# Second mixture of a two-layer transformer kernel: gate and up of the first 512 tokens move ahead of two turned groups and the router's products

## The chip, the cores and the metric

The kernel runs on one core of a Trainium2 chip. The metric is the device time of one launch in microseconds (us), given as the median over runs. A profile is one execution taken by the hardware profiler. Its engines are PE (matmuls; PEld are its weight loads), ACT (ScalarE), DVE (VectorE), POOL (GpSimd) and SP, the queue that issues the DMAs. L86 means line 86 of the kernel.

## The reference, cut to what matters

Two layers, each an attention and a mixture of experts, with a layer norm behind each of the four parts. Activations are 2 x 1024 tokens of 256 features, float32. The part touched here is what lies between the attention of the second layer and its mixture:

```
x = _layernorm(x + _L1_attn_ref(x, ...), axis=-1)
# _L1_ffn_ref:
scores = xf @ gate_w.T
probs = jax.nn.softmax(scores.astype(jnp.float32), axis=-1)
_, idx = jax.lax.top_k(probs + gate_b, TOP_K)          # 6 of 16 experts
h = jax.nn.silu(xf @ W1.T + B1) * (xf @ W3.T + B3)     # each expert, and the shared one
out = h @ W2.T + B2
```

## The kernel before, in words

**Data.** Features lie on the 128 partitions, tokens along the free axis. Every float32 operand of a product is split into a rounded high part and a remainder (`xh`, `xl`; `hi_gu`, `lo_gu`), and `mm3` forms each product as three matmuls (L86, L87, L88). ACT rounds (copies) and DVE subtracts to get the remainder; for weights POOL does the subtraction (L1190).

**A mixture.** `mixture` is called twice, as "f0" for the first layer and "f1" for the second. It runs over `2 * NT` tiles of hidden units K (the two halves of 1024 tokens one after the other), and for each K over NC = 2 chunks c of 512 tokens. PE's order for a (K, c) is `gate(K, c)`, `up(K, c)` (twelve matmuls together), then `down(K - 1, c)`, then the side tasks that `plan` names for this place. ACT does silu, DVE the product with up (`f_hid`, L1473), ACT the rounding (`f_hh`, L1422), DVE the remainder (`f_hl`, L1484). `gate(0, 1)` waits for silu of (0, 0), and `up(0, 1)` for the product of (0, 0), as there is one bank of PSUM for gate and one for up.

**Side tasks.** The norm and the router of 1024 tokens are cut into tasks, each with a part on PE (`tensor`), ACT (`scalar`) and DVE (`vector`), and each engine does its parts in program order. Engines meet through the semaphores of a ring: `filled` by PE, `rounded` by ACT, `emptied` by DVE. The tasks that count here:
- `root`: ACT takes the square root (L212), DVE the reciprocal (L223) and then normalises eight blocks of 128 tokens into `yT` (L227). Each block is counted on `xn_done`.
- `nb` s, s = 0 to 3: 256 tokens, called a group here, are turned back so that features lie on partitions. PE does four 128x128 turns (L204), ACT copies them to `xh` (L217), DVE subtracts to `xl` (L241) and counts `emptied`.
- `lg` c: the router's scores of 512 tokens, six matmuls with `g_rw_gwh` and `g_rw_gwl`. PE waits until `nb` 2c + 1 is emptied. DVE copies the result out (L389).
- `lt`: PE turns the scores (eight small turns, L347); it waits until the copy of `lg` 1 is done. DVE goes on with the maximum (L392 to L395).

**The start of f1.** What is called `lead` in the program, and `fore` inside `mixture`, is the list `root`, `nb` 0 to 3, `lg` 0, `lg` 1. With `ready` = 0, PE does all of it ahead of the loop over K, then gate and up of (0, 0), then `lt`, the first task of `plan[0, 0]`, and then gate of (0, 1). ACT does `root`, rounds the first weights (L1186), and then does its parts of the other six tasks, loads the table of silu (L1435), rounds `b2` (L1438) and goes on to silu (L1411). DVE does all its parts of the list, then `b2l` (L1492), then the product of (0, 0).

In the call for f0 (`ready` = 2, `split` = 2) PE does two tasks of `fore` ahead of the loop and the rest behind gate and up of (0, 0).

Of the kernel before, what the change touches and what calls it, by code (L numbers as in the profile page):

```python
# [1190 lines left out]
                           ALU.subtract).then_inc(self.lo_done, 1)  # L1191


def mixture(nc, tag, counters, w, gu, ready, xh, xl, yT, idr, eps, psum, shared_gate, routers, fore, split, plan, after, begins=(), store=None):

# [9 lines left out]
    with Phase(nc, tag, psum) as ph:  # L1207
# [42 lines left out]
        fore_ring = Ring(counters, side_banks + [o for row in y_banks for o in row] + [up_ps, gate_ps])  # L1250
# [65 lines left out]
        @block.tensor  # L1316
        def _(pe):
            def gate(K, c):
                if c == 0:
                    pe.wait_ge(gu.lo_done, K + 1)  # L1320
                if K * NC + c >= 1:

                    pe.wait_ge(silu_done, K * NC + c)
                elif fore_ring.last(gate_ps):
                    pe.wait_ge(fore_ring.emptied, fore_ring.last(gate_ps))
                for dt in range(DT):
                    w0 = dt * P
                    i = mm3(pe, gate_ps, hi_gu[:, K % 2, w0:w0 + P], lo_gu[:, K % 2, w0:w0 + P],
                            xh[:, dt, tokens(K, c)], xl[:, dt, tokens(K, c)], dt == 0, dt == DT - 1)
                i.then_inc(gate_done, 1)  # L1330

            def up(K, c):
                if K * NC + c >= 1:

                    pe.wait_ge(prod_done, K * NC + c)
                elif fore_ring.last(up_ps):
                    pe.wait_ge(fore_ring.emptied, fore_ring.last(up_ps))
                for dt in range(DT):
                    w0 = (DT + dt) * P
                    i = mm3(pe, up_ps, hi_gu[:, K % 2, w0:w0 + P], lo_gu[:, K % 2, w0:w0 + P],  # L1340
                            xh[:, dt, tokens(K, c)], xl[:, dt, tokens(K, c)], dt == 0, dt == DT - 1)
                i.then_inc(up_done, 1)

            def begin_y(K, c):
                half = K // NT
                if half:

                    pe.wait_ge(y_kept, (c + 1) * DT)
                for dt in range(DT):
                    if not half and fore_ring.last(y_banks[dt][c]):  # L1350
                        pe.wait_ge(fore_ring.emptied, fore_ring.last(y_banks[dt][c]))
                    pe.matmul(y_banks[dt][c], idr[:], xh[:, dt, tokens(K, c)], start=True, stop=False)
                    pe.matmul(y_banks[dt][c], idr[:], xl[:, dt, tokens(K, c)], start=False, stop=False)

            def bias_y(K, c):
                r, x = routers[K // NT], slice(c * CH, (c + 1) * CH)
                pe.wait_ge(b2_lo, 1)
                for dt in range(DT):
                    d = slice(dt * P, (dt + 1) * P)
                    mm3(pe, y_banks[dt][c], b2h[:, d], b2l[:, d], r.cTh[:, x], r.cTl[:, x], False, False)  # L1360

            def down(K, c):
                if c == 0:
                    pe.wait_ge(lo_dn_done, K + 1)
                pe.wait_ge(hlo_done, K * NC + c + 1)
                for dt in range(DT):
                    d0 = dt * P
                    i = mm3(pe, y_ps[:, dt, c, :], hi_dn[:, K % 2, d0:d0 + P], lo_dn[:, K % 2, d0:d0 + P],
                            hh[:, K % 2, c, :], hl[:, K % 2, c, :], False, K % NT == NT - 1)
                i.then_inc(down_done, 1)  # L1370

            for side, t in fore[:split] if ready else fore:
                side.tensor(pe, t, fore_ring)
            for K in range(2 * NT + 1):
                for c in range(NC):
                    if K <= LAST:
                        gate(K, c)
                        up(K, c)
                    if ready and K == 0 and c == 0:
                        for side, t in fore[split:]:  # L1380
                            side.tensor(pe, t, fore_ring)
                    if K >= 1:
                        if (K - 1) % NT == 0:
                            begin_y(K - 1, c)
                        if biased and (K - 1) % NT == nsh:
                            bias_y(K - 1, c)
                        down(K - 1, c)
                    for side, t in plan.get((K, c), ()):
                        side.tensor(pe, t, ring)
# [509 lines left out]
def program(nc, a, out):  # L1899
    with ExitStack() as stack:  # L1900
# [5 lines left out]
        xh = sb("xh", [P, DT, T], F32R)  # L1906
        xl = sb("xl", [P, DT, T], F32R)
        yT = sb("yT", [P, DT, T])
        ident = sb("ident", [P, P])
        idr = sb("idr", [P, P], F32R)  # L1910
        eps = sb("eps", [P, 1])
        psum = stack.enter_context(nc.psum_tensor("psum", [P, 8, CH], F32))
        rows = out.rearrange("b s d -> (b s) d")
        counters = Counters(nc, stack)
# [8 lines left out]
        def maps(r):  # L1923
            return ([(r, ("ct", c)) for c in range(S // CH)] +
                    [(r, ("cm", c, m)) for c in range(S // CH) for m in range(r.rw.nmap)])
# [16 lines left out]
        def place(first, slots):  # L1942
# [3 lines left out]
        w0 = {"groups": 1, "shared_tiles": NSH0, "topk": 2, "gate_w": a["gw0"], "gate_b": None, "sel": a["sel0"],  # L1946
              "gu": a["gu0"], "bias": a["bias0"], "down": a["down0"]}
# [4 lines left out]
        with Phase(nc, "g") as g:  # L1952
# [19 lines left out]
            with Phase(nc, "x") as x:  # L1972
                wqkv = Projection(x, "wqkv", a["wqkv1"], a["bqkv1"])
                x.level(0)
                ks = [x.sb("ks0", [P, 2, S], F32R)]
                vs = [x.sb("vs0", [P, S // P, G1, VW])]
                qhi = [x.sb("qhi0", [P, 2, S], F32R)]
                qlo = [x.sb("qlo0", [P, 2, S], F32R)]
                with Phase(nc, "s0") as s:
                    n0b, n1a = norm(s, "n0b", 1), norm(s, "n1a", 0)  # L1980
                    r0b = router(s, "r0b", 1, rw0, "n0b")
                    kv, khi, klo = s.sb("kv", [P, S]), s.sb("khi", [P, S], F32R), s.sb("klo", [P, S], F32R)
                    x0 = QKVHalf(s, "x0", 0, wqkv, kv, khi, klo, xh, xl, ident, "n1a").into(qhi[0], qlo[0], ks[0], vs[0])
                    plan = {**place(0, norm_slots(n0b) + PAUSE + router_slots(r0b)),
                            **place(NT0 + 1, norm_slots(n1a) + PAUSE + tasks(x0, PROJECT))}
                    for c, t in enumerate(maps(r0a)[3::2]):
                        plan[3, c] = plan.get((3, c), []) + [t]
                    mixture(nc, "f0", counters, w0, gu0, 2, xh, xl, yT, idr, eps, psum, True, (r0a, r0b), maps(r0a)[:2] + maps(r0a)[2::2], 2, plan, n1a, (wqkv, x0))

                ks.append(x.sb("ks1", [P, 2, S], F32R))  # L1990
                vs.append(x.sb("vs1", [P, S // P, G1, VW]))
                qhi.append(x.sb("qhi1", [P, 2, S], F32R))
                qlo.append(x.sb("qlo1", [P, 2, S], F32R))
                x.level(0)
                queries = Queries(x, "queries", qhi, qlo)
                with Phase(nc, "s1") as s:
                    n1b = norm(s, "n1b", 1)
                    kv, khi, klo = (o[:].rearrange("p s n -> p (s n)") for o in (raw_gu, hi_gu, lo_gu))
                    x1 = QKVHalf(s, "x1", 1, wqkv, kv, khi, klo, xh, xl, ident, "n1b").into(qhi[1], qlo[1], ks[1], vs[1])
                    in_turn(nc, "p1", counters, psum, tasks(n1b, FORE + [("root",)] + BACK) + tasks(x1, PROJECT), (x1, wo, rw1, queries))  # L2000
                    o1a = OutHalf("o1a", 0, wo, z[0], qhi[0], qlo[0], xh, xl, yT, ident, idr)
                    follows(n2a, o1a)
                    order = [TURN[0], TURN[1], GATHER[0], GATHER[1], TURN[2], TURN[3], GATHER[2], GATHER[3]]
                    rear = list(zip((1, 2, 4, 6, 8, 9, 11, 13, 15, 17, 19, 21), tasks(o1a, order) + tasks(n2a, FORE)))
                    grouped_attention(nc, "a1", counters, queries, (x0, x1), ks, vs, z, ident, psum, rear)

            with Phase(nc, "s2") as s:
# [12 lines left out]
                        **place(NSH1, tasks(o1b, TURN) + PAUSE + tasks(o1b, GATHER) + PAUSE + norm_slots(n2b) + PAUSE +  # L2020
                                router_slots(r1b)),
                        **place(NT1 + 1, norm_slots(n3a, False))}
                mixture(nc, "f1", counters, w1, gu1, 0, xh, xl, yT, idr, eps, psum, False, (r1a, r1b), lead, 1, plan, n3a, (),
                        (n3a, rows, stored, 0))
            n3b = norm(g, "n3b", 1)
            in_turn(nc, "p3", counters, psum, tasks(n3b, FORE + [("root",)]), (), (n3b, rows, stored, NormHalf.GROUPS))
# [86 lines left out]
```

## Time and profile before

| | us |
|---|---|
| median of 3 runs | 2165.48 (2164.84 to 2167.04) |
| the profiled execution | 2165.89 |
| its span, first to last instruction | 2163.9 |
| PE busy in it | 2092.4 |
| mean granted clock of PE | 0.984 of full |

Times in the rows are in us from the start of the span. A row of the timeline gives the start, the duration, the engine, the line, the operation, what is written and read, the shape and the count; in square brackets stands how long the engine had been idle and which instruction released it. Matmuls overlap, so the distance between two starts is what one costs.

### The profile page before, as it was taken

What the parts mean: (1) busy time and instruction counts of PE and PEld (TensorE: products, weight loads), DVE (VectorE), ACT (ScalarE), POOL (GpSimd) and SP (SyncE); (2) the same over time, 40 slices, a digit from 0 to 9 for tenths busy, and PEclk for the clock granted to TensorE, in tenths of its full rate; (3) what the DMA queues carried; (4) which work ended last, traced back from release to release, by engine and by line L of the source; (5) the groups of instructions that cost most, each with busy time, mean ns of one, the idle gap of its engine ahead of it and who ended that gap; (6) DMA issues with size and microseconds to landing.
All of it is one profiled execution on the core that took longest, in us unless ns stands there. A gap on an engine that the chain in (4) does not pass through costs nothing. (4 is left out here: it accounts for less than half of the span.)

```text
span 2163.9 us, 31289 instructions
## 1 busy us (share of the span) xinstructions
PE 2092.4 (97%) x11136; PEld 1595.3 (74%) x11136; DVE 1454.1 (67%) x2761; ACT 1211.4 (56%) x2435; POOL 576.7 (27%) x679
## 2 busy tenths in 40 slices
PE   7999999999999999989999989999999899999997
PEld 6888888888788888877788863333334678778886
DVE  5666666667666776666656568888885556655555
ACT  5666666666556666644444444778777534444433
POOL 3444444444334444422222210000000112222221
PEclk9999999999999999999999986999999999999999
DMA  2000000000000000011111120000000111111111
GB/s 74 20 21 19 14 21 20 21 20 20 9 20 21 21 20 21 16 30 39 45 44 45 44 50 14 20 18 22 16 22 2 43 37 44 44 44 39 50 52 56
DMA packets 54301, 64.78 MB, mean 30 GB/s; under 512 B 9179, under 2 KB 34566, under 8 KB 54150
## 3 DMA queue, kind: packets, MB, share of 16 engines
q1 hardware_dynamic: 54150, 62.81, 10.4%
q8 instruction: 90, 1.47, 0.3%
q14 instruction: 61, 0.50, 0.1%
HBM read 52.68 MB, written 2.10 MB: 25 GB/s over the span
## 5 line engine op out<-in xcount | busy, mean ns | idle before, releaser
L862 POOL TENSOR_TENSOR a_pr<-a_pr,a_rinv 128x512 f32<-128x512 f32 (+3 forms) x384 | 312.2, 827 | 476.4 <-DVE a_rinv L1109 476.4
L86 PE MATMUL psum<-xh,g_hi_gu 128*128 128x512 f32 x928 | 377.7, 407 | 16.2 <-DVE xl L1092 10.0
L88 PE MATMUL psum<-xh,g_lo_gu 128*128 128x512 f32 x928 | 363.3, 392 | 0.0
L87 PE MATMUL psum<-xl,g_hi_gu 128*128 128x512 f32 x928 | 362.6, 391 | 0.0
L1817 DVE TENSOR_REDUCE a_negm<-psum 128x1 f32<-128x1024 f32 x256 | 301.6, 1220 | 37.5 <-PE psum L1688 36.8
L1190 POOL TENSOR_TENSOR g_lo_gu<-g_raw_gu,g_hi_gu 128x512 fp32r<-128x512 f32 x84 | 108.6, 1292 | 793.3 <-ACT g_hi_gu L1186 793.3
L1796 ACT ACTIVATE a_pt<-psum 128x512 f32<-128x512 f32 x512 | 269.2, 603 | 85.5 <-PE psum L1703 85.0
L1484 DVE TENSOR_TENSOR f_hl<-f_hid,f_hh 128x512 fp32r<-128x512 f32 x168 | 116.9, 696 | 238.6 <-ACT f_hh L1422 236.6
L1411 ACT ACTIVATE f_act_s<-psum,g_gu_bias 128x512 f32<-128x512 f32 x168 | 115.0, 684 | 277.4 <-PE psum L88 277.1
L1014 ACT ACTIVATE a_pr<-psum,a_negm 128x128 f32<-128x128 f32 (+7 forms) x256 | 190.0, 742 | 106.8 <-DVE a_negm L1099 102.6
L1021 ACT ACTIVATE a_pth<-psum 128x512 fp32r<-128x512 f32 (+3 forms) x384 | 174.7, 489 | 113.2 <-PE psum L921 107.9
L86 PEld LDWEIGHTS psum<-xh,g_hi_gu 128*128 128x128 f32 x928 | 174.8, 188 | 56.8 <-issue 14.4
L88 PEld LDWEIGHTS psum<-xh,g_lo_gu 128*128 128x128 f32 x928 | 174.5, 188 | 38.4
L1116 DVE TENSOR_TENSOR a_ptl<-psum,a_pth 128x512 fp32r<-128x512 f32 (+3 forms) x384 | 201.1, 551 | 1.5 <-ACT a_pth L1021 1.2
L87 PEld LDWEIGHTS psum<-xl,g_hi_gu 128*128 128x128 f32 x928 | 175.3, 189 | 31.8
L1422 ACT ACTIVATE f_hh<-f_hid 128x512 fp32r<-128x512 f32 x168 | 105.5, 628 | 157.7 <-DVE f_hid L1478 153.6
L1688 PE MATMUL psum<-x_ks,x_queries_qq 48*128 48x512 f32 x512 | 185.9, 474 | 7.9 <-DVE a_negm L1817 4.7
L1099 DVE CUSTOM_DVE_ANT_0 psum<-psum,a_mask 128x128 f32<-128x128 f32 (+7 forms) x256 | 191.7, 749 | 1.5 <-PE psum L88 0.2
L921 PE MATMUL psum<-ident,a_pr 128*128 128x128 f32 x1152 | 170.5, 275 | 9.8 <-DVE a_ptl L1116 7.0
L1703 PE MATMUL psum<-x_queries_qq,x_ks 49*128 49x512 f32 x512 | 171.5, 481 | 0.9 <-ACT a_pt L1796 0.4
L1703 PEld LDWEIGHTS psum<-x_queries_qq,x_ks 49*128 49x128 f32 x512 | 68.4, 188 | 133.1 <-ACT a_pt L1796 127.2
L921 PEld LDWEIGHTS psum<-ident,a_pr 128*128 128x128 f32 x1152 | 134.3, 140 | 33.0 <-POOL a_pr L862 21.3
(298 smaller groups left out, 4310.0 us busy)
## 6 DMA issues: line engine op xcount, KB each, us to landing
g_raw_gu<-in_gu SPq DMA_DIRECT2D x84, 256.0 KB, 2.7
f_raw_dn<-in_down SPq DMA_DIRECT2D x84, 128.0 KB, 2.0
g_raw_gu<-in_qkv SPq DMA_DIRECT2D x32, 256.0 KB, 2.9
a_wvr<-in_qkv SPq DMA_DIRECT2D x32, 128.0 KB, 2.3
a_wor<-in_o SPq DMA_DIRECT2D x32, 128.0 KB, 2.0
x_queries_qq<-x_qhi SPq DMA_DIRECT2D x128, 32.0 KB, 2.0
yT<-in_xT SPq DMA_DIRECT2D x4, 512.0 KB, 6.6
x_queries_qq<-x_qlo SPq DMA_DIRECT2D x64, 32.0 KB, 2.0
```

Of the source, the lines that this page charges most:

```text
L86: pe.matmul(out, a_hi, b_hi, start=first, stop=False)
L87: pe.matmul(out, a_hi, b_lo, start=False, stop=False)
L88: return pe.matmul(out, a_lo, b_hi, start=False, stop=last)
L862: pool.tensor_tensor(x, x, rinv[:, j:j + 1].to_broadcast([P, count * P]), ALU.mult).then_inc(p_done, 1)
L921: i = pe.transpose(t_ps[:, n % 2, k * P:(k + 1) * P], pr[qt % NP][:, (k0 + k) * P:(k0 + k + 1) * P], ident[:])
L1014: act.activation(split(qt, pr[qt % NP][:, 0:n]), scored(qt), ACT.Exp, bias=negm[:, qt % NP:qt % NP + 1], scale=-1.0, accum_out=rsum[:, qt ...
L1099: dve.tensor_tensor_reduce(x, x, split(qt, mask[:, S - (qt + 1) * P:S]), -1.0, 3.0e38, ALU.add, ALU.min, negm[:, qt % NP:qt % NP + 1]).the ...
L1116: dve.tensor_tensor(ptl[c][:, p, :], t_ps[:, n % 2, 0:count * P].rearrange("p (k q) -> p k q", q=P), pth[c][:, p, :].bitcast(F32), ALU.sub ...
L1688: m = pe.matmul(mx_ps[:, bank, half, :], qq[p0:p0 + ROWS, u % QSLOT, g % 2, q * P:(q + 1) * P], ks[b][p0:p0 + ROWS, g % 2, half * CH:(half ...
L1703: pe.matmul(st_ps[:, n % 3, :], ks[b][p0:p0 + ROWS + 1, g % 2, kt * P:(kt + 1) * P], qq[p0:p0 + ROWS + 1, u % QSLOT, g % 2, :], start=True ...
L1796: act.activation(pt[:, s % SLOTS, g, :], st_ps[:, n % 3, :], ACT.Exp, scale=1.0 / HD1).then_inc(exp_done, 1)
L1817: dve.tensor_reduce(negm[:, u % 2, g * NQ + q:g * NQ + q + 1], mx_ps[:, bank, :, :], AX.XY, ALU.max, negate=True).then_inc(mx_taken, 1)
```

## The change

`mixture` gets a parameter `ahead`: how many tasks of `fore` PE does before the loop over K. The rest follow gate and up of (0, 0) in both calls. For f0 `ahead` is 2, as `split` is, so its order stays; the added wait is only issued where the last task ahead is an `nb`, and there it is a `ct`. For f1 `ahead` is 3: `root`, `nb` 0 and `nb` 1 stand ahead, then PE waits until DVE has emptied `nb` 1 (tokens 0 to 511 are complete then), then come gate and up of (0, 0), and behind them `nb` 2, `nb` 3, `lg` 0, `lg` 1 and `lt`. The orders of ACT, DVE, POOL and SP are not edited; `split` still divides ACT's list.

```diff
-def mixture(nc, tag, counters, w, gu, ready, xh, xl, yT, idr, eps, psum, shared_gate, routers, fore, split, plan, after, begins=(), store=None):
+def mixture(nc, tag, counters, w, gu, ready, xh, xl, yT, idr, eps, psum, shared_gate, routers, fore, split, ahead, plan, after, begins=(), store=None):
...
-            for side, t in fore[:split] if ready else fore:
+            for side, t in fore[:ahead]:
                 side.tensor(pe, t, fore_ring)
+            for side, t in fore[:ahead][-1:]:
+                if t[0] == "nb":
+                    pe.wait_ge(fore_ring.emptied, fore_ring.count((side.name, t)))
             for K in range(2 * NT + 1):
                 for c in range(NC):
                     if K <= LAST:
                         gate(K, c)
                         up(K, c)
-                    if ready and K == 0 and c == 0:
-                        for side, t in fore[split:]:
+                    if K == 0 and c == 0:
+                        for side, t in fore[ahead:]:
                             side.tensor(pe, t, fore_ring)
...
-                    mixture(nc, "f0", counters, w0, gu0, 2, xh, xl, yT, idr, eps, psum, True, (r0a, r0b), maps(r0a)[:2] + maps(r0a)[2::2], 2, plan, n1a, (wqkv, x0))
+                    mixture(nc, "f0", counters, w0, gu0, 2, xh, xl, yT, idr, eps, psum, True, (r0a, r0b), maps(r0a)[:2] + maps(r0a)[2::2], 2, 2, plan, n1a, (wqkv, x0))
...
-                mixture(nc, "f1", counters, w1, gu1, 0, xh, xl, yT, idr, eps, psum, False, (r1a, r1b), lead, 1, plan, n3a, (),
+                mixture(nc, "f1", counters, w1, gu1, 0, xh, xl, yT, idr, eps, psum, False, (r1a, r1b), lead, 1, 3, plan, n3a, (),
```

## Rows read from the trace of the kernel before

**Rows 1.** The page: busy tenths of PE in 40 slices, and its granted clock.

```profile
PE   7999999999999999989999989999999899999997
...
PEclk9999999999999999999999986999999999999999
```

**Rows 2.** PE's waits over the span: for what, us in total, times, longest.

```profile
PE psum L204 <- DVE yT L227: 8.6, 3, 4.6
```

**Rows 3.** Timeline of PE at the start of f1, and DVE's first product.

```profile
1690.59 1.97 PE L204 MATMUL psum<-ident,yT 128*128 128x128 f32 x8 [3.69 <-DVE yT L227]
...
1692.88 1.97 PE L204 MATMUL psum<-ident,yT 128*128 128x128 f32 x8 [0.32 <-DVE yT L227]
...
1694.81 0.58 PE L86 MATMUL psum<-xh,g_rw_gwh 128*16 128x512 f32 x1
...
1696.05 0.40 PE L86 MATMUL psum<-xh,g_rw_gwh 128*16 128x512 f32 x1
...
1697.90 0.39 PE L88 MATMUL psum<-xh,g_rw_gwl 128*16 128x512 f32 x1
...
1700.62 0.39 PE L88 MATMUL psum<-xh,g_lo_gu 128*128 128x512 f32 x1
...
1700.94 0.67 PE L347 MATMUL psum<-ident,yT 16*128 16x16 f32 x8
...
1701.12 0.75 DVE L1473 SCALAR_TENSOR_TENSOR f_hid<-psum,g_gu_bias,f_act_s 128x512 f32<-128x512 f32 x1 [1.78 <-PE psum L88]
...
1701.54 0.50 PE L86 MATMUL psum<-xh,g_hi_gu 128*128 128x512 f32 x1
```

**Rows 4.** Timeline of POOL, DVE and ACT in the same stretch.

```profile
1691.40 1.27 POOL L1190 TENSOR_TENSOR g_lo_gu<-g_raw_gu,g_hi_gu 128x512 fp32r<-128x512 f32 x1 [419.73 <-ACT g_hi_gu L1186]
...
1693.39 1.96 DVE L241 TENSOR_TENSOR xl<-psum,xh 128x512 fp32r<-128x512 f32 x3
...
1694.88 0.60 ACT L217 ACTIVATE xh<-psum 128x512 fp32r<-128x512 f32 x1 [0.26 <-PE psum L204]
...
1695.49 1.28 ACT L1435 ACT_TABLE_LOAD   x1
1695.51 0.69 DVE L241 TENSOR_TENSOR xl<-psum,xh 128x512 fp32r<-128x512 f32 x1 [0.16 <-ACT xh L217]
...
1698.33 0.68 DVE L389 COPY yT<-psum 16x512 f32<-16x512 f32 x1 [0.69 <-PE psum L88]
```

**Rows 5.** Timeline of the stage before the grouped attention, turns and ACT's copies.

```profile
1268.81 1.94 PE L198 MATMUL psum<-ident,yT 128*128 128x128 f32 x16 [1.43 <-PEq L54]
...
1269.47 2.06 ACT L217 ACTIVATE yT<-psum 128x512 f32<-128x512 f32 x4 [0.97 <-PE psum L198]
...
1275.33 3.68 PE L204 MATMUL psum<-ident,yT 128*128 128x128 f32 x16 [4.59 <-DVE yT L227]
```

**Rows 6.** Stretches: length, busy per engine (instructions), PE's granted clock, DMA share, GB/s.

```profile
1279.60:1280.00 0.40, 0.40 (x3) 0.32 (x3) 0.32 (x1) 0.04 (x1) 0.00 (x0) 0.96 0.28 56
1290.00:1337.00 47.00, 40.00 (x100) 16.95 (x102) 38.63 (x35) 10.10 (x20) 0.00 (x0) 0.53 0.14 25
...
1689.00:1690.00 1.00, 0.00 (x0) 0.00 (x0) 0.41 (x2) 0.51 (x2) 0.00 (x0) 0.62 0.77 274
...
1696.00:1697.00 1.00, 1.00 (x6) 0.41 (x5) 0.25 (x2) 0.99 (x3) 0.00 (x0) 0.97 0.00 0
...
2149.50:2156.80 7.30, 3.54 (x22) 2.72 (x22) 2.87 (x13) 5.20 (x9) 0.00 (x0) 1.00 0.00 0
```

**Rows 7.** Timeline of PE at the kernel's start.

```profile
10.03 0.77 PE L86 MATMUL psum<-xh,g_hi_gu 128*128 128x512 f32 x1 [10.03 <-DVE xl L1092]
...
13.15 0.46 PE L87 MATMUL psum<-xl,g_hi_gu 128*128 128x512 f32 x1
...
13.45 0.39 PE L88 MATMUL psum<-xh,g_lo_gu 128*128 128x512 f32 x1
```

**Rows 8.** The stretch from gate of (0, 1) to nearly the end of f1.

```profile
1701.50:2150.00 448.50, 443.96 (x1974) 358.65 (x1974) 256.76 (x434) 186.75 (x335) 100.32 (x99) 1.00 0.15 45
```

## The prediction

> **What bounds the kernel now.** I read four views. First the page: the matmul engine (PE) is at 9 tenths in nearly every slice, so a change pays only where PE idles, and costs wherever it puts an idle stretch in front of PE [rows 1]. Second, PE's waits over the whole run: the second largest is the one for `yT` from L227, the normalised rows which the turning back needs, 8.6 us in three places [rows 2]. The second mixture `f1` begins with one of them. Third, the timeline of PE there [rows 3]: groups 0 and 1 are turned from 1690.59, groups 2 and 3 from 1692.88, and the router's twelve products (`lg`, 16 columns of weights, but 512 moving columns) start at 1694.81. They are followed without a gap by gate and up of the first 512 tokens, by `lt` at 1700.94 and by gate of the second 512 tokens, G, at 1701.54. Fourth, the other engines in that stretch [rows 4]. VectorE (DVE) forms `xl` of groups 0, 1 and 2 back to back from 1693.39 (three in 1.96 us, so 0.64 apart); group 1's ends at 1693.39 + 0.64 + 0.68 = 1694.71. PE starts 0.1 us behind that. So what ends PE's wait is DVE's second subtraction, and two things lie under it for nothing: the turns of groups 2 and 3, which PE does while DVE is busy, and, under the later lg products, ScalarE's (ACT's) copies and DVE's subtractions of these groups. Likewise DVE's copy of the second lg result (1698.33 to 1699.01) lies under gate and up. I follow one mark, G: from there on the order on every engine is unchanged.
>
> **The change, part by part.** In the first mixture the third and later tasks stay where they were, and the new wait isn't issued (the task ahead is no `nb`): 0. In `f1` no product, copy, transfer or byte is added. SyncE's and GpSimd's queues are untouched. One semaphore wait is added on PE, for DVE's subtraction of group 1. Queued behind it are now gate, up, and then everything else of PE. Before, `lg` 0 waited for the very same event, so gate can't start before 1694.81, and its weights are ready (GpSimd is done at 1691.40 + 1.27 = 1692.67) [rows 4]. Gain from an earlier start of PE: nothing. What changes is what is covered.
>
> Step 1, twelve gate and up products from 1694.81. At full clock they are 0.227 us apart ((1700.62 - 1697.90) / 12). If the clock rises when it did before, three steps take 1.24 us (1694.81 to 1696.05), the other eight 1.82, and the last starts at 1697.87. The next task starts 0.32 later, as `lt` did (1700.62 to 1700.94): T = 1698.19 [rows 3].
>
> Step 2, groups 2 and 3 are turned from T, now alone. At full clock sixteen turns take 1.94 us, so eight take about 0.95; ACT's first copy starts 0.66 after the first turn, and four copies take 2.06, so they are 0.49 apart [rows 5]. The second copy ends at T + 0.66 + 0.49 + 0.60 = T + 1.75. DVE follows 0.03 behind each (as at 1695.51), 0.64 apart and 0.68 long: done at T + 2.61. PE follows 0.07 later, so `lg` 1 starts at T + 2.68. `lg` 0 covers part of it (from T + 0.97, six products at 0.23, to T + 2.35); 0.33 us stay open.
>
> Step 3, `lg` 1: five steps, with 0.1 for the first one after a wait, put its last product at T + 3.93. DVE's copy starts 0.43 behind it (1697.90 to 1698.33) and takes 0.68: T + 5.04. `lt` needs it and has no cover now: it starts at about T + 5.1, and G comes 0.60 later, at T + 5.7 [rows 3, 4]. PE waits some 1.0 us here, where it waited for nothing before.
>
> Step 4, ACT and DVE behind the moved tasks. ACT ends the copies at T + 1.75, loads the table (1.28), does the two small ones, and is free at about T + 3.5, before the silu of G is needed; silu ends at T + 4.2. DVE has the first product behind both lg copies and `b2l`: about T + 5.35, which is 0.35 before G, where before it was 0.42 before G (1701.12) [rows 3]. Nothing new is late: 0, but nothing is won either.
>
> At the old clock the sum is G = 1698.19 + 5.7 = 1703.9, that is 2.35 later: about 0.95 for the turns, 0.33 and 1.0 for the two open waits, the rest for restarts. A lower bound of this part is 1.3 (both waits hidden somehow), the upper one 2.6.
>
> Step 5, the clock. PE is at the lower of its levels (1.2 GHz) from 1689.2 (the mean of 0.62 in the slice from 1689 puts the fall there), after it stood idle behind the attention, and at 2.4 GHz from 1696.0 [rows 6]. It had then been turning and multiplying since 1690.59, 5.4 us with two gaps of 0.3. After the change PE turns two groups, then stands for 2.3 us until 1694.81. Three rises give the bounds: 3.1 us after the first product at the kernel's start (10.03 to 13.15), 4.3 after the first turn in the stage before the grouped attention (1275.33 to 1279.6), and 5.4 here [rows 5, 6, 7]. Counted from 1694.81 that is 1697.9, 1699.1 or 1700.2. A slow step takes 0.41 here and 0.45 at the kernel's start; I use 0.42. The middle value makes eleven of the twelve products slow: last start 1694.81 + 10 x 0.42 + 0.38 = 1699.4, T = 1699.7, G = 1705.4, 3.85 us later than before. The early one gives T = 1699.2 and 3.3; the late one all twelve slow, and half-rate turns behind them, 4.3.
>
> The rule that bears on it is in the Trainium skill, "TensorE: Matmul & The Clock Gate", Part 1: the slow level is the default, and only sustained work releases the fast one. The rows of rises agree; by it the sum is the 3.85 above. Its Part 4 says more: a turn doesn't count as work for the clock. By this the rise would stay where it was, and the sum be 2.35. That is the second rival.
>
> The sum is +3.8 us. The profiled execution took 2165.89 us for a span of 2163.9, and stands 0.4 above the median of 2165.48. On the median the forecast is 2169.3; the new profile should show a span near 2167.7. A difference of 0.2% (4.3 us) is about what a measurement of this kernel can tell from no change, so this loss most likely counts as none.
>
> **Rivals.**
> A, the forecast: cover lost and clock late, +3.3 to +4.3.
> B, the clock rises as early as before. For it: counted from the first ordinary product, the rise came 1.2 us later here (1694.81 to 1696.0) and in the earlier stage it came 0.6 us after the sixteen turns had ended (1275.33 + 3.68 = 1279.0, to 1279.6). Against it: from 1290 to 1337 PE was busy 85% with ordinary products and the clock stayed at 0.53, so a short run of products is not enough; and at the kernel's start it took 3.1 us [rows 5 to 7]. Time: 2165.48 + 2.35 = 2167.8.
> C, the clock rises and then falls again in the new waits (0.33 and 1.0 us, with tiny turns between). The stay at the low level here lasted 6.8 us (1689.2 to 1696.0); a second one costs 6.8 x (1 - 0.227 / 0.42) = 3.1. Time 2165.5 + 3.8 + 3.1 = 2172.4, slower. Against it: at 2149.5 to 2156.8 PE was busy only half of the stretch (3.54 of 7.30) and kept the full clock; the new stretch is busier [rows 6].
> D, the other side: the loss is given back. Silu of the first tokens is done 1.5 us before G, so ACT and DVE could run ahead of PE, and the waits that PE has later in this mixture (448.50 - 443.96 = 4.54 us idle) would shrink [rows 8]. If all go, -4.5 + 3.8 = -0.7: 2164.8. It decides from the point where more than 3.8 of the 4.5 vanish. Against it: DVE's first product stays behind the lg copies (step 4), 0.35 before G instead of 0.42, and both engines are in order from there.
> E, the change has less effect than it seems, because the turns of groups 2 and 3 overlap gate and up somehow: excluded, as PE issues in program order and they stand behind `up`.
>
> **How the numbers follow.** A 0.74, B 0.13, C 0.09, D 0.04. Faster by over 0.2%: a part of D and scatter, 0.03. Slower: C (0.09) and the upper third of A, since 4.3 is its late end and runs of one kernel spread by 2 us (2164.84 to 2167.04): 0.25; together 0.34. Within 0.2%: 0.63. The likeliest is 2169.3. The range takes in B's time with some scatter below, 2167.0, and A's late end with scatter and a part of C above, 2171.3.
>
> **What would show it.** In the new profile: PE's first gate product of `f1` at the place where lg was, 1.3 us after DVE's first L241; a wait of PE of some 2.3 us ahead of it in place of 0.3 and 0.3; the turns of groups 2 and 3 about 4.9 us behind it, about 1 us long; `lt` 5.1 us behind the turns with a wait for DVE's L389 of about 1.0; and G 10.6 us behind the first gate product (6.73 from the first lg product before). The granted clock should rise 3 to 5.5 us after the first gate product. From G to the end the time should be unchanged within 0.5 us (462.4 us before, 2163.9 - 1701.54). The prediction is wrong if gate starts earlier than DVE's second subtraction, if the copy L389 doesn't delay `lt`, if the clock rises within 2 us, or if the idle time of PE after G changes by more than 1 us.

## The result, and the profile after

The changed kernel takes 2170.45 us (median of 16 runs, 2167.51 to 2172.82), the kernel before 2166.4 us (16 runs, 2164.84 to 2167.87). The ratio is 1.0017, 95% interval 1.001 to 1.0023: 4.05 us more, where 3.8 were forecast. The profiled execution took 2170.44 us for a span of 2168.4. Two executions far out of line, 8848.66 us in the first experiment and 5099.13 us of the kernel before beside it, are in no ratio and no spread given below, and no trace shows what they did.

First the timeline of PE in the changed kernel, with ACT's square root on top. It answers to [rows 3].

```profile
1689.14 0.30 ACT L212 ACTIVATE g_n2a_std<-g_n2a_mv,eps 128x8 f32<-128x8 f32 x1
...
1690.51 1.97 PE L204 MATMUL psum<-ident,yT 128*128 128x128 f32 x8 [3.70 <-DVE yT L227]
1694.59 0.79 PE L86 MATMUL psum<-xh,g_hi_gu 128*128 128x512 f32 x1 [2.12 <-DVE xl L241]
1695.18 0.63 PE L87 MATMUL psum<-xl,g_hi_gu 128*128 128x512 f32 x1
...
1699.45 0.63 PE L88 MATMUL psum<-xh,g_lo_gu 128*128 128x512 f32 x1
1699.88 1.47 PE L204 MATMUL psum<-ident,yT 128*128 128x128 f32 x8
1701.10 0.47 PE L86 MATMUL psum<-xh,g_rw_gwh 128*16 128x512 f32 x1
...
1703.01 0.39 PE L86 MATMUL psum<-xh,g_rw_gwh 128*16 128x512 f32 x1 [0.28 <-DVE xl L241]
...
1704.16 0.39 PE L88 MATMUL psum<-xh,g_rw_gwl 128*16 128x512 f32 x1
1705.41 0.64 PE L347 MATMUL psum<-ident,yT 16*128 16x16 f32 x8 [0.86 <-DVE yT L389]
1705.98 0.50 PE L86 MATMUL psum<-xh,g_hi_gu 128*128 128x512 f32 x1
```

The order is the new one. The brackets name three waits that the change brought: 2.12 us for DVE's second subtraction (L241), 0.28 for its fourth, and 0.86 for the copy of the second router result (L389). All twelve gate and up products have a duration of 0.63 or more and, behind the first, stand 0.43 apart, so all of them are slow. The mark G, gate of the second 512 tokens, stands at 1705.98.

Next ACT and DVE behind the moved tasks, from the same timeline. It answers to [rows 4].

```profile
1700.94 1.09 ACT L217 ACTIVATE xh<-psum 128x512 fp32r<-128x512 f32 x2 [7.83 <-PE psum L204]
...
1701.58 1.29 DVE L241 TENSOR_TENSOR xl<-psum,xh 128x512 fp32r<-128x512 f32 x2 [7.04 <-ACT xh L217]
...
1704.59 0.68 DVE L389 COPY yT<-psum 16x512 f32<-16x512 f32 x1 [1.14 <-PE psum L88]
...
1705.53 0.73 DVE L1476 SCALAR_TENSOR_TENSOR f_hid<-psum,g_gu_bias,f_act_s 128x512 f32<-128x512 f32 x1
```

ACT and DVE stood idle for 7.8 and 7.0 us until the turns of groups 2 and 3 came. DVE's first product starts 0.45 ahead of G (0.42 before), so these engines did not get ahead of PE.

Last the granted clock (the third number from the end) around its fall and rise, and the long rest of the mixture. It answers to [rows 6, 8].

```profile
1690.00:1691.00 1.00, 0.49 (x3) 0.49 (x4) 1.00 (x4) 0.43 (x1) 0.00 (x0) 0.76 0.78 172
...
1700.00:1701.00 1.00, 1.00 (x8) 1.00 (x7) 0.00 (x0) 0.06 (x1) 0.00 (x0) 0.62 0.00 0
...
1705.94:2154.44 448.50, 443.97 (x1974) 358.53 (x1974) 256.67 (x434) 186.70 (x335) 100.37 (x99) 1.00 0.15 45
```

A mean between the two levels, 0.50 and 1.00, tells where the clock changed: it fell at 1690.52 and rose at 1700.76. The low stretch was 10.2 us long, against 6.8 in the kernel before. The last row is the stretch from G on, as long as the one in [rows 8]: PE is busy for 443.97 of it, where it was 443.96. Nothing that lies behind G moved.

Because the whole trace can be shifted by something earlier, I measure from the start of the square root (L212), A, to the first gate product of tile 1, H. Before, A is 1689.22 and H 1704.39: 15.17 us. After, A is 1689.14 and H 1708.87: 19.73. The difference is 4.56 us. From H to the end both kernels need 459.5 us, and so does every kernel below (459.44 to 459.69).

### The profile page after: what moved, and what is told of

It is laid out like the page before. It is cut to its first block and busy times, and to the rows that moved or that the text cites. A ratio compares the mean times of both kernels' runs of the same rounds, so it can differ in the third digit from the quotient of the medians.

```text
span 2168.4 us, 31290 instructions
## 1 busy us (share of the span) xinstructions
PE 2095.3 (97%) x11136; PEld 1597.4 (74%) x11136; DVE 1453.3 (67%) x2761; ACT 1211.1 (56%) x2435; POOL 577.4 (27%) x679
```

## The experiments

| kernel | A to H | low clock, from A | ratio to before (95%) |
|---|---|---|---|
| before | 15.17 | 0.0 to 6.8 | |
| before again | 15.01 | -0.4 to 6.4 | |
| changed | 19.73 | 1.4 to 11.6 | 1.0017 (1.001 to 1.0023) |
| changed again | 19.17 | 0.2 to 10.4 | |
| changed again | 19.09 | 0.0 to 10.2 | |
| e1, turns ahead | 16.02 | -0.4 to 6.4 | 1.0002 (0.9992 to 1.0012) |
| e3, gap filled | 17.28 | -0.4 to 6.4 | 1.0009 (1.0 to 1.0018) |
| e4, PE kept busy | 16.88 | none | 1.0005 (0.9996 to 1.0014) |
| e6, lt between | 18.18 | -0.5 to 9.8 | 1.0012 (1.0003 to 1.0021) |
| e7, both covers | 15.13 | -0.2 to 6.6 | 1.0002 (0.9992 to 1.0012) |
| e5, before, PE kept busy | 14.66 | none | 1.0 (0.9991 to 1.0008) |
| e8, before, weights later | 14.88 | 0.1 to 7.0 | 0.9995 (0.9986 to 1.0004) |
| e9, before, both | 13.66 | none | 0.9988 (0.9979 to 0.9996) |

The runs of one kernel spread by 3 to 9 us, so effects of 1 us are read from A to H, and the ratios only say whether they contradict it. Each A to H is from one profiled execution. Those of the kernel before differ by 0.16, those of the changed kernel by 0.64, with where the clock fell; a difference of 0.2 or less shows nothing.

**The turns ahead of gate again.** For f1 `ahead` is 5, and PE still waits for group 1 only.

```diff
-            for side, t in fore[:ahead][-1:]:
+            for side, t in fore[:3][-1:]:
...
-                ... False, (r1a, r1b), lead, 1, 3, plan, n3a, (),
+                ... False, (r1a, r1b), lead, 1, 5, plan, n3a, (),
```

> The changed kernel, but the turns of groups 2 and 3 stand ahead of gate again (still only the wait for group 1); the router's products stay behind gate and up. I measure from the start of the square root L212 to the first gate product of tile 1 (A to H): 15.17 us before, 19.73 after the change. Three-term theory (turns without cover and their wait 1.3, wait for the copy L389 1.0, clock 1.5 to 2.1): only the second term is left, as the turns keep PE at work before the products: A to H 16.1, time 0.9 us above the kernel before, 3.6 below the changed one. Rival (the loss comes with the router's products moving, whatever the turns do, and the clock is late by itself): A to H 18 or more.

A to H is 16.02, as the theory had it. PE turns groups 2 and 3 while DVE subtracts, its first gate product starts at A + 5.49, and the first line is its only new wait. The slices show the clock's fall and rise:

```profile
1703.32 0.65 PE L347 MATMUL psum<-ident,yT 16*128 16x16 f32 x8 [0.86 <-DVE yT L389]
...
1690.00:1691.00 1.00, 0.00 (x0) 0.00 (x0) 0.00 (x0) 0.99 (x2) 0.00 (x0) 0.67 0.50 141
1697.00:1698.00 1.00, 1.00 (x6) 0.82 (x5) 0.69 (x1) 0.98 (x2) 0.00 (x0) 0.92 0.00 0
```

The rival is out: moving the router's products behind gate and up costs just the cover of their copy. Against the repeated run of the kernel before, whose clock fell at the same distance from A, that is 16.02 - 15.01 = 1.0 us.

**The gap filled.** Five products of 512 columns, which nothing uses, stand on PE ahead of the wait. They read tokens that don't change here and write a bank that `up` overwrites.

```diff
+            def idle_products(n):
+                for _ in range(n if not ready else 0):
+                    pe.matmul(up_ps, idr[:], xh[:, 0, S:S + CH], start=True, stop=True)
...
+            idle_products(5)
             for side, t in fore[:ahead][-1:]:
```

> The changed kernel with five products of 512 columns, which nothing uses, on PE in the gap between the turns of group 1 and the wait for DVE. Same outputs. If the late clock comes from the idle gap, the clock rises 4.3 to 5.4 us after the first turn as in the kernel before, at most three to four gate products are slow, and A to H falls from 19.73 to 17.1 to 17.7; the median falls by about 2.4 us to 1.0010 of the kernel before. Rival (the rise would come late in any case, by the state of the chip at that moment or because the turned groups are missing): A to H stays at 19 to 20.

Timeline of PE and two slices of its clock in this kernel:

```profile
1691.35 1.97 PE L204 MATMUL psum<-ident,yT 128*128 128x128 f32 x8 [3.70 <-DVE yT L227]
1692.97 2.48 PE L1374 MATMUL psum<-xh,idr 128*128 128x512 f32 x5
1695.44 0.80 PE L86 MATMUL psum<-xh,g_hi_gu 128*128 128x512 f32 x1
...
1689.00:1690.00 1.00, 0.00 (x0) 0.00 (x0) 0.00 (x0) 0.99 (x2) 0.00 (x0) 0.79 0.36 47
1696.00:1697.00 1.00, 1.00 (x5) 0.80 (x4) 0.00 (x0) 0.00 (x0) 0.00 (x0) 0.79 0.00 0
```

The clock rose at 1696.42 (a mean of 0.79 means that 0.42 of the slice was at 0.50), 1.0 us after the first gate product, and A to H fell by 2.45 us to 17.28, or by 1.8 to 1.9 against the two repeats of the changed kernel below. Work that computes nothing made this stretch shorter. That the idle gap is the cause of the late clock, and not the moment at which the clock fell, is shown by e6 below: its PE does the same as the changed kernel up to the rise, its clock fell 0.45 us ahead of A (0.40 here), and it rose at A + 9.8 instead of A + 6.4. The ratio fell from 1.0017 to 1.0009, as expected, though the intervals overlap.

**PE kept busy throughout.** Eleven such products at the start of the mixture, nine in the gap.

```diff
+            idle_products(11)
             for side, t in fore[:ahead]:
                 side.tensor(pe, t, fore_ring)
+            idle_products(9)
```

> The changed kernel with eleven unused products of 512 columns at the start of this mixture (PE idles there while ACT and DVE prepare the norm) and nine in the gap, so that PE hardly idles and the clock should not fall. This takes the clock out of the sum: theory A to H 16.9 to 17.0, of which 1.8 above the kernel before is lost cover (turns and two waits) minus the three slow products that the kernel before has too. Rival (the waits are worth less, the clock was nearly all of the loss): A to H at or below 15.5. Rival (the clock was little): 18.5 or more.

```profile
1685.79 2.74 PE L1374 MATMUL psum<-xh,idr 128*128 128x512 f32 x11 [1.07 <-PEq L54]
1688.42 1.30 PE L204 MATMUL psum<-ident,yT 128*128 128x128 f32 x8
1689.48 2.33 PE L1374 MATMUL psum<-xh,idr 128*128 128x512 f32 x9
1692.54 0.50 PE L86 MATMUL psum<-xh,g_hi_gu 128*128 128x512 f32 x1 [0.74 <-DVE xl L241]
```

The granted clock is 1.00 in every slice here. A to H is 16.88. That leaves the order alone, and both of this run's rivals are out.

**lt between gate and up.** PE's order only.

```diff
                         gate(K, c)
+                        if not ready and (K, c) == (0, 1):
+                            for side, t in plan[0, 0]:
+                                side.tensor(pe, t, ring)
                         up(K, c)
...
-                    for side, t in plan.get((K, c), ()):
+                    for side, t in plan.get((K, c), ()) if ready or (K, c) != (0, 0) else ():
```

> The changed kernel, but PE does lt between gate and up of the second 512 tokens instead of ahead of gate; the orders of ACT and DVE stay. Then gate (1.4 us) covers DVE's copy of the second result, for which lt waits. Theory: that wait (0.86 in the profile, 1.0 with the restart) vanishes: A to H from 19.73 to 18.7, the median 1.0 us lower. Rival (another wait, for silu or for the first product, takes its place): A to H 19.4 to 19.8.

```profile
1704.24 0.40 PE L88 MATMUL psum<-xh,g_rw_gwl 128*16 128x512 f32 x1
1704.54 0.50 PE L86 MATMUL psum<-xh,g_hi_gu 128*128 128x512 f32 x1
...
1706.13 0.67 PE L347 MATMUL psum<-ident,yT 16*128 16x16 f32 x8
1706.73 0.50 PE L86 MATMUL psum<-xh,g_hi_gu 128*128 128x512 f32 x1
...
1689.00:1690.00 1.00, 0.00 (x0) 0.00 (x0) 0.00 (x0) 1.00 (x1) 0.00 (x0) 0.80 0.23 68
1699.00:1700.00 1.00, 1.00 (x4) 0.75 (x3) 0.00 (x0) 0.00 (x0) 0.00 (x0) 0.58 0.00 0
```

The wait is gone, and no other took its place. A to H fell by 1.55 us, more than the 1.0 expected, because the clock in this run also rose earlier (A + 9.8, not 11.6), as the slices show. Counted from the start of the last router product, so without the clock, H comes 4.0 us later where it was 4.7: the reordering is worth 0.7.

**Both covers.** The edits of the first and the fourth experiment together.

> The changed kernel with both repairs that leave gate and up of the first 512 tokens ahead of the router's products: the turns of groups 2 and 3 ahead of gate, and lt between gate and up of the second 512 tokens. Both waits and the idle gap are gone. Theory: A to H 15.2 to 15.4, as the kernel before (15.17), and its time. So the move itself wins nothing. Rival (gate first does save something once its waits are gone): 14.7 or less.

15.13, against 15.17 and 15.01 for the kernel before, and 0.9 less than the first experiment alone. With its losses repaired, gate ahead of the router's products wins nothing that these profiles can show; the forecast of 15.2 to 15.4 was 0.1 too high.

**Both kernels once more.**

> The changed kernel once more, to see how far the clock moves the mark from run to run. If the low stretch is 10.1 us long in it whenever PE idles in the gap, and only its start varies against the square root L212 (-0.3 to +1.6 us in the runs so far), A to H lies between 18.9 and 19.8. If the low stretch can also be 6.8 us long in this kernel, A to H can be 17.3.

> As the run before it: 18.9 to 19.8 if the low stretch is 10.1 us again, 17.3 if it can be short.

> The kernel before once more: a low stretch of 6.8 us, starting between -0.3 and +1.6 us from the square root; A to H 14.9 to 15.8.

Slices of the first of these, with its fall and rise:

```profile
1688.00:1689.00 1.00, 0.00 (x0) 0.00 (x0) 0.20 (x1) 0.74 (x2) 0.00 (x0) 0.82 0.83 174
1698.00:1699.00 1.00, 1.00 (x4) 0.77 (x3) 0.00 (x0) 0.00 (x0) 0.00 (x0) 0.56 0.00 0
```

19.17 and 19.09 for the changed kernel, 15.01 for the other. The low stretch was 10.2 us again in both runs of the changed kernel and 6.8 in the one before; only its start moved.

**The kernel before, PE kept busy; weights rounded later; both.** The first has `idle_products(11)` ahead of `fore`. The second is one number, `split`: ACT rounds the first weights behind group 1's copy.

```diff
-                ... False, (r1a, r1b), lead, 1, plan, n3a, (),
+                ... False, (r1a, r1b), lead, 3, plan, n3a, (),
```

> The kernel before with eleven unused products of 512 columns at the start of the second mixture, where PE idles 3.7 us. If the clock then doesn't fall, the three slow router products become fast: A to H (square root L212 to the first gate product of tile 1) from 15.17 to 14.6, the time 0.6 us lower, which a measurement can hardly tell. If the idle stretch is not what lowers the clock: 15.2.

> The kernel before, but ACT rounds the first weights behind the copy of group 1 instead of ahead of group 0 (split 3 for 1). GpSimd's subtraction L1190 then no longer runs beside DVE's normalisation L227, of which one block took 1.41 us in place of 0.41. Theory: the long block is due to GpSimd running beside it; DVE's second subtraction and the router's first product come 0.8 us earlier, but two more products are slow, as the clock rises at the same time: A to H from 15.17 to 14.4 to 14.8. Rival (the long block has another cause, or gate now waits for its weights): 15.2 or more.

> Both edits in the kernel before: eleven unused products at the start, and the first weights rounded later. They should add up, as no product is slow then: A to H 13.8, the time 1.4 us (0.06%) below the kernel before. If the earlier start is eaten up by slow products or by the weights: 14.6.

DVE's normalisation in the kernel before and then in the second of these, each as count, shortest, median and longest in ns:

```profile
L227 DVE TENSOR_SCALAR yT<-yT,g_n2a_mv,g_n2a_rstd x8: 403/409/1407, 1689.8 to 1693.1; 128x256 f32<-128x256 f32 x8
```

```profile
L227 DVE TENSOR_SCALAR yT<-yT,g_n2a_mv,g_n2a_rstd x8: 404/406/414, 1688.8 to 1691.1; 128x256 f32<-128x256 f32 x8
```

The long block is gone with GpSimd's subtraction moved. The first router product comes at A + 4.83 instead of 5.59, 0.76 earlier, but A to H falls by only 0.29, to 14.88, a little above the expected 14.4 to 14.8: five products are slow now instead of three. In the third kernel, where the clock doesn't fall, the same edit is worth 14.66 - 13.66 = 1.0. Its time is 2163.28 us against 2165.92, ratio 0.9988 (0.9979 to 0.9996): the interval lies below 1, so it beats the kernel before, which the changed kernel does not, and A to H falls by 1.51, more than the 0.51 and 0.29 of the two edits alone. The medians differ by 2.64, more than this stretch explains; the rest is not shown.

## Why the prediction was right

**Where gate can start.** Forecast: not before DVE's second subtraction, no gain. Measured: 1694.59 with a wait of 2.12 us for exactly that; against A it is 0.14 us earlier than the router's first product was.

**Lost cover.** Forecast: 2.35 us, as 0.95 for the turns, 0.33 and 1.0 for the two waits. With the clock taken out of both kernels it is 16.88 - 14.66 = 2.22. Its parts: the turns with their wait 17.28 - 16.02 = 1.26 (the two runs' clocks fell and rose at the same places), against 1.28 forecast; the wait for the copy 1.0, against 1.0.

**The clock.** This is the term that was too small. Forecast: 1.5, with eleven slow products and a rise 4.3 us after the first; it rose 6.2 us after it (1694.59 to 1700.76), beyond the late bound of 5.4. All twelve products were slow, the first 0.59 from the second, and so were most of the turns behind them, from which `lg` 0 started 1.22 us later instead of 0.97. Against the filled gap the term is 19.73 - 17.28 = 2.45 in the profiled execution, and 1.9 and 1.8 in the two repeats. The twelve products with their step to the turns took 5.29 where 4.89 were forecast, and from the turns to G it was 6.10 where it was 5.7, while gate started 0.14 earlier: so 3.85 became 4.56 in this profile. In the repeats it was 3.9 to 4.0 against 15.17. The median difference of 4.05 agrees with the repeats.

The direction of this term held, its rule did not. The forecast let the rise follow the first gate product at a distance taken from three other rises (3.1 to 5.4 us). It came 6.2, 5.0 and 4.8 us behind that product in the three profiles of the changed kernel and 4.3 in e6; what was the same in all four was the length of the low stretch, 10.2 us. So the size depended on where the fall happened to lie, and part of the good agreement of 3.8 with 4.05 is luck: the cover was forecast 0.13 too high, the clock 0.3 to 0.95 too low.

**Rival B** (clock back as early as before) fell: both kernels had products of 512 columns from the same time on, 5.5 us behind A, and the filled gap alone brought the early rise back. **Rival C** (a second fall in the new waits) did not occur: the clock stayed at 1.00 through both. **Rival D** (given back later) fell on the last row above: 443.97 against 443.96. **Step 4** (ACT and DVE not late, not early) held, 0.45 against 0.35 forecast.

Forecast +3.8 with 2167.0 to 2171.3, measured 2170.45; a loss of 0.17% lies inside the bound of 0.2% that was to be told from no change, though with 16 runs its interval excludes 1.

## What to carry to other kernels

Before moving work ahead of a wait, ask what that wait already hides: here PE turned two groups and multiplied for the router under DVE's work, and the earlier place of the big products bought nothing, since the old first product had waited for the same event. Count the gap that opens as clock, too: 2 us of idle PE behind a short burst cost as much again as the lost cover. And look at what runs beside the operation that ends the wait; none of the orders of PE's tasks tried here beat the kernel before, while moving one GpSimd instruction gave 1.0 us where the clock was kept up (0.29 where it fell, which the noise of these profiles nearly covers).

## What the runs showed of the hardware

**The low stretch has two lengths.** In the ten profiled executions in which the clock fell here it stayed at 1.2 GHz for 6.8 us (six times: before, before again, e1, e3, e7, e8) or 10.2 us (four times: the changed kernel three times and e6), and nothing between, while its start lay between 0.5 us before A and 1.4 us after. It was 6.8 wherever PE worked nearly without a break from its first turn on, and 10.2 wherever it idled 2.1 us behind the first eight turns. How many products were slow followed from the start alone, and moved A to H of the changed kernel between 19.09 and 19.73.

**Turns count as work for the clock.** The first experiment and the changed kernel differ on PE, up to the rise, in eight turns alone; gate starts at A + 5.49 and A + 5.45. With these turns the clock rose at A + 6.4 (in the five profiled executions that have them and in which it fell, by A + 7.0), without them and with nothing in their place at A + 9.8 to A + 11.6. The closest pair is e1 and e6, whose clocks fell 0.43 and 0.45 us ahead of A: the rise came at A + 6.4 and at A + 9.8. The Trainium skill, "TensorE: Matmul & The Clock Gate", Part 4, says that transposes don't count in the same way. For these float32 turns the runs say they do.

**GpSimd beside DVE.** One block of L227 took 1.41 us instead of 0.41 while GpSimd subtracted 128 x 512 elements in SBUF, and none did once that ran elsewhere. ACT's rounding of the weights moved with it, but it is not the cause: it ended at 1691.32 (1690.69 + 0.63), GpSimd worked from 1691.40 to 1692.67, and DVE was in one single block all through the stretch below (its length, DVE busy and its instructions, PE's granted clock, DMA share, GB/s):

```profile
1691.60:1692.40 0.80, 0.80 (x1) 0.50 0.55 191
```

The subtraction L241, which has one operand in SBUF and one in PSUM, was not slowed beside it. Four of them took 2.48 us in e9 (first two lines), with GpSimd at work beside them, and 2.47 in e5 (last two), where GpSimd had ended before they began:

```profile
1690.86 2.48 DVE L241 TENSOR_TENSOR xl<-psum,xh 128x512 fp32r<-128x512 f32 x4
1691.59 1.28 POOL L1190 TENSOR_TENSOR g_lo_gu<-g_raw_gu,g_hi_gu 128x512 fp32r<-128x512 f32 x1 [421.19 <-ACT g_hi_gu L1186]
...
1691.12 1.27 POOL L1190 TENSOR_TENSOR g_lo_gu<-g_raw_gu,g_hi_gu 128x512 fp32r<-128x512 f32 x1 [419.42 <-ACT g_hi_gu L1186]
1693.10 2.47 DVE L241 TENSOR_TENSOR xl<-psum,xh 128x512 fp32r<-128x512 f32 x4
```

The Trainium skill, "GPSIMD Engine Reference", section 1, names this contention for DVE's instructions in a mode with two ports or with two inputs in SBUF. L241 is neither, and agrees; in which mode L227 ran no trace here shows, and the price, one microsecond for one block, is this trace's.
